# A graph-network kernel's edge loop rewritten: variance by cross terms, one vector pass, fp32 row strips, a ring of four halves, the reciprocal root on GpSimd

## The chip, the cores and the metric

The kernel runs on one core of one Trainium2 chip. The metric is device microseconds (us) of one execution. Two timed executions of the kernel before gave 4982.13 and 4989.26 us, median 4985.69 us.

Engines are called PE (TensorE matmul), PEld (its weight load), DVE (VectorE), ACT (ScalarE), POOL (GpSimd) and SP (SyncE, which issues DMAs).

## The reference, cut to what matters

Two message-passing layers over 12,500 nodes and 200,000 edges sorted by destination. The part that the change rewrites is the first layer's edge work:

```python
def _L0_gnn_ref(x, edge_index, edge_attr, W1, b1, g1, be1, W2, b2, Wu, bu, gu, beu):
    row, col = (edge_index[0], edge_index[1])
    msg_in = jnp.concatenate([x[row], edge_attr], axis=-1)      # 128 + 32 columns
    h = msg_in @ W1 + b1                                        # 256 columns
    h = jax.nn.gelu(_layernorm(h, g1, be1), approximate=False)
    msg = h @ W2 + b2
    agg = jax.ops.segment_sum(msg, col, num_segments=x.shape[0])
    u = jnp.concatenate([x, agg], axis=-1) @ Wu + bu
    u = jax.nn.gelu(_layernorm(u, gu, beu), approximate=False)
    return u + x
...
h = jnp.maximum(_layernorm(x, axis=-1), 0.0)
x = x + _L0_gnn_ref(h, edge_index, edge_attr_32, ...)
h = jnp.maximum(_layernorm(x, axis=-1), 0.0)
x = x + _L1_gnn_ref(h, edge_index, ...)                         # hypergraph layer
```

Since the message's second product is linear, the kernel sums gelu(layernorm(h)) per destination node and multiplies by W2 Wu afterwards.

## The kernel before, in words

The program is thirteen phases with a barrier between them: `setup_phase`, `node_tables`, `edge_messages`, `far_messages`, and so on up to `output_rows`. Each phase is written out by hand, engine by engine: every engine runs its instructions in the order of its block, and semaphores (`s_...`) order the engines against each other. No scheduler is involved.

`node_tables` works on 14 groups of 7 tiles of 128 nodes. It normalises x, multiplies by the x part of W1 (already centred, so that a row's mean is zero) and stores a table `p_tab` of 256 columns per node, which the edge loop gathers from. It also splits the 32 edge features (fp32) into three bf16 parts and stores them.

`edge_messages` is the edge loop. A tile is 128 edges, a **half** is 8 tiles, and there are 196 halves. For a half H, before the change:

- SP loads indices, digits and six bf16 blocks of edge features.
- POOL (`half`) gathers 8 x 128 rows of `p_tab` with 8 indirect DMAs (L561); every second gather waits until DVE has consumed the two tiles of the half before that stood in the same buffer (`s_add`). Between them it takes the power -0.5 of the variances, 128x8 (L567).
- PE (`product`) multiplies features by weights with two bf16 matmuls for a tile (L601, L602).
- DVE adds product and gathered rows (L752), scales by the root and g1 (L768) and adds be1 (L774).
- ACT squares and sums each tile for the variance (L674), applies gelu (L680) and builds one-hot masks for a histogram (L692 to L701).
- PE (`window_sums`, L623) multiplies the 256 hidden columns of a tile (as stationary operand, 128x128 fp32 twice) by a 128x32 one-hot mask of the destinations in a window of 32 nodes; DVE (`keep`, L791) adds the result to the sums in memory. PE also adds the histogram (L609).

The engines work on different halves at once: PE multiplies features of half H+1 while window sums of H-1 and H-2 run.

`node_update` (L1356 to L1474) multiplies the sums by W2 Wu, 14 groups of 7 tiles, and makes the second layer's input.

## Time and profile before

| what | us |
|---|---|
| median of 2 timed executions | 4985.69 |
| span of the profiled execution (the profile gives no other time of it) | 5038.3 |
| `setup_phase`, 0 to 39.6 | 39.6 |
| `node_tables`, to 346.8 | 307.2 |
| `edge_messages`, to 3111.5 | 2764.7 |
| far edges and degrees, to 3405 | 293.5 |
| `node_update`, to 3657 | 252.0 |
| the second layer, to the end | 1381.3 |

The profiled execution is one run and 52.6 us (1.1%) longer than the median of the timed ones. The stage bounds are read from the first and last instructions of each phase (the gathers of L561 begin at 346.8, the last `keep` ends with the loop at about 3111.5). Engine busy times are sums over a stretch; a wait that an engine spends for another is printed in brackets behind the instruction that ended it, with the line that released it. PEclk is the granted TensorE clock in parts of 2.4 GHz, so that 0.50 is its lower level of 1.2 GHz.

### The profile page before, as it was taken

The numbers are of one execution on the slowest core, as the hardware profiler recorded it, in microseconds if no ns is written. First come the engines' busy times: TensorE is split into PE (matmuls) and PEld (weight loads), VectorE is DVE, ScalarE is ACT, GpSimd is POOL, SyncE is SP. The second block draws the span as 40 slices with busy tenths as digits, with TensorE's granted clock in tenths as the row PEclk, the third lists the DMA queues.
The fourth block names the chain that finished last, engine by engine and source line by source line (L and its number), as shares of the span: only waits on it lengthen the run. The fifth ranks groups of instructions, "written<-read, shape, count | busy, mean of one in ns | idle before, by whom it ended". The sixth has DMA issues, their size and how long they took to land. (4 is left out here: it accounts for less than half of the span.)

```text
span 5038.3 us, 84982 instructions
## 1 busy us (share of the span) xinstructions
PE 3638.0 (72%) x16168; PEld 2611.6 (52%) x16168; DVE 2939.9 (58%) x8166; ACT 2492.2 (49%) x7380; POOL 3210.0 (64%) x2574
## 2 busy tenths in 40 slices
PE   3438999999999999999999997567633336666600
PEld 1216666666666666666666665565523324444300
DVE  6776776777777777767667775556811113323237
ACT  2437777777777777777777774462200001222200
POOL 2337777777777777777777774102366656888842
PEclk8665555555555555555555555555555555555555
DMA  6964444444444444444444442003311114555558
GB/s 249 343 242 113 117 117 112 115 114 114 117 112 116 113 116 115 114 114 115 111 112 113 116 113 61 12 15 95 101 49 47 44 38 80 75 74 78 74 124 222
DMA packets 726546, 557.03 MB, mean 111 GB/s; under 512 B 278174, under 2 KB 657170, under 8 KB 724594
## 3 DMA queue, kind: packets, MB, share of 16 engines
q0 software_dynamic: 135328, 250.63, 21.7%
q1 hardware_dynamic: 585138, 305.55, 21.4%
q10 hardware_dynamic: 6048, 0.52, 0.1%
q14 instruction: 24, 0.20, 0.0%
q8 instruction: 8, 0.13, 0.0%
HBM read 420.83 MB, written 135.45 MB: 110 GB/s over the span
## 5 line engine op out<-in xcount | busy, mean ns | idle before, releaser
L561 POOL DMA_INDIRECT stage<-p_tab,indices x1568 | 1761.6, 1123 | 660.3 <-issue 468.6
L674 ACT ACTIVATE table_weights_and_bias<-stage 128x256 bf16<-128x256 f32 x1568 | 632.4, 404 | 369.1 <-DVE stage L752 202.1
L768 DVE SCALAR_TENSOR_TENSOR stage<-stage,rstd,g 128x256 f32<-128x256 f32 x1568 | 653.9, 480 | 213.1 <-POOL rstd L567 213.1
L601 PE MATMUL ps_tiles<-edge_weights_a,edge_features_a 128*128 128x256 bf16 x1568 | 611.9, 390 | 201.1 <-DVE stage L752 156.4
L623 PE MATMUL ps_b<-window_mask,stage 128*128 128x32 f32 x3136 | 725.2, 402 | 2.9 <-ACT stage L680 2.9
L623 PEld LDWEIGHTS ps_b<-window_mask,stage 128*128 128x128 f32 x3136 | 698.3, 327 | 46.2 <-issue 43.3
L623 PE MATMUL ps_a<-window_mask,stage 128*128 128x32 f32 x3136 | 718.7, 400 | 1.9 <-ACT stage L680 1.7
L623 PEld LDWEIGHTS ps_a<-window_mask,stage 128*128 128x128 f32 x3136 | 706.8, 330 | 2.5 <-ACT stage L680 2.4
L602 PE MATMUL ps_tiles<-edge_weights_b,edge_features_b 64*128 64x256 bf16 x1568 | 614.4, 392 | 0.0
L752 DVE TENSOR_TENSOR stage<-ps_tiles,stage 128x512 f32<-128x512 f32 x784 | 538.1, 687 | 104.6 <-issue 101.2
L680 ACT ACTIVATE stage<-stage 128x1024 f32<-128x1024 f32 x392 | 414.2, 1057 | 366.8 <-DVE stage L774 332.5
L1713 POOL DMA_INDIRECT acc<-stage,target x320 | 502.6, 1571 | 105.7 <-ACT stage L1769 72.5
L774 DVE TENSOR_TENSOR stage<-stage,be 128x1024 f32<-128x1024 f32 x392 | 478.4, 1220 | 0.1
L692 ACT ACTIVATE high_mask<-iota,digits 128x98 bf16<-128x98 f32 x1568 | 436.8, 361 | 0.0
L601 PEld LDWEIGHTS ps_tiles<-edge_weights_a,edge_features_a 128*128 128x128 bf16 x1568 | 164.4, 105 | 484.4 <-issue 282.2
L1544 POOL DMA_INDIRECT stage<-xp_tab,indices x320 | 307.3, 960 | 160.1 <-issue 93.5
L741 DVE TENSOR_TENSOR window_mask<-iota,digits 128x256 f32<-128x256 f32 x196 | 83.4, 425 | 471.6 <-remote 376.7
L602 PEld LDWEIGHTS ps_tiles<-edge_weights_b,edge_features_b 64*128 64x128 bf16 x1568 | 158.7, 101 | 350.0 <-issue 350.0
L567 POOL TENSOR_TENSOR rstd<-var,minus_half 128x8 f32<-128x8 f32 x197 | 330.2, 1676 | 12.9 <-DVE var L760 8.6
L1763 ACT COPY sums<-ps_c 32x256 f32<-32x256 f32 x80 | 28.7, 358 | 547.6 <-PE ps_c L1733 543.4
L674 ACT ACTIVATION_READ_ACCUMULATOR table_weights_and_bias<-stage 128x1 f32 x1568 | 292.2, 186 | 0.0
L1560 PE MATMUL ps_a<-window_mask,stage 128*128 128x32 f32 x320 | 89.3, 405 | 256.7 <-DVE window_mask L1576 102.2
(258 smaller groups left out, 5413.2 us busy)
## 6 DMA issues: line engine op xcount, KB each, us to landing
edge_features_a<-ea_part SPq DMA_DIRECT2D x784, 64.0 KB
ea_part<-sums SPq DMA_DIRECT2D x42, 896.0 KB, 5.5
sums<-ea_d SPq DMA_DIRECT2D x14, 1792.0 KB, 9.2
stage<-p_tab,indices POOLq DMA_INDIRECT x1568
edge_features_b<-ea_part SPq DMA_DIRECT2D x392, 64.0 KB
acc<-zeros_bf SPq DMA_DIRECT2D x392, 64.0 KB
sums<-acc SPq DMA_DIRECT2D x56, 448.0 KB
sums<-src_d SPq DMA_DIRECT2D x46, 512.0 KB
```

What stands on the lines that cost most here:

```text
L561: gp.indirect_dma_start(out=rows[:, j, :], out_offset=None, in_=k.p_tab[:, :], in_offset=bass.IndirectOffsetOnAxis(ap=k.meta[h][:, j:j + 1 ...
L567: gp.tensor_tensor(k.rstd[i][:, :], k.var[i][:, :], k.neghalf[:, 0:HALF], ALU.pow)\
L601: nc.tensor.matmul(psH[q][:, t, :], k.eaA[h][:, e:e + P], k.wA[:, :], start=True, stop=False)
L602: nc.tensor.matmul(psH[q][:, t, :], k.eaB[h][:, e:e + P], k.wB[:, :], start=False, stop=True).then_inc(s_tile, 1)
L623: last = nc.tensor.matmul(psU[g][:, q, c, :], left, right, start=i == 0, stop=i == 1)
L674: nc.scalar.activation(k.scratch[:, j % GROUP, :], z[h][:, j, :], ACT.Square, scale=HID ** -0.5, accum_out=k.ssq[i][:, at:at + 1]).then_in ...
L680: nc.scalar.activation(part, part, ACT.Gelu).then_inc(s_gelu, 1)
L692: last = nc.scalar.activation(k.hi[h][:, j, :], k.iota[:, 0:NT], ACT.Square, bias=k.digits[h][:, 2 * HALF + j:2 * HALF + j + 1])
L752: v.tensor_tensor(z[h][:, 2 * q:2 * q + 2, :], psH[q], rows[:, 2 * q:2 * q + 2, :], ALU.add).then_inc(s_add, 1)
L768: o(v.scalar_tensor_tensor(z[h][:, j, :], z[h][:, j, :], root, k.g1[:, :], ALU.mult, ALU.mult))
L774: v.tensor_tensor(part, part, k.be1[:, :].unsqueeze(1).to_broadcast([P, GROUP, HID]), ALU.add).then_inc(s_z, 1)
L1713: gp.indirect_dma_start(out=k.acc[r], out_offset=bass.IndirectOffsetOnAxis(ap=k.target[h][:, j:j + 1], axis=0), in_=summed[:, r, :], in_of ...
```

## The change

The edge loop is rewritten on every engine, and tables and memory are laid out for it.

- **Cross terms.** The variance of a hidden row is split into a part of the node alone (computed in `node_tables` by ACT, and stored in `p_tab`), a cross term and a part of the features alone. `p_tab` grows from 256 to 292 columns (`PW`), and comes already multiplied by g1. PE multiplies features by a 128x128 block matrix (`feature_products`), DVE adds 32 gathered cross columns, multiplies by the features and reduces to 128x8 (`variance`). ACT's squares are gone from the edge loop.
- **One DVE pass.** The features are scaled by the root before the product (`scale_features`), turned on PE (`turn`), copied by ACT (`take_turned`), and multiplied by the weights (`feature_part`), where be1 is added as three bf16 parts. DVE then makes hidden = gathered row x root + product in one instruction a tile (`hidden`, L915).
- **fp32 row strips.** `feature_part` uses 32 of the array's 128 rows for a tile: four tiles stand on the four strips, fp32, with outputs in four PSUM banks. The bf16 parts of the features and their stores are gone from `node_tables`.
- **Ring of four halves.** The gathered rows have four buffers and hidden is written in place. A gather into a buffer waits for the window sums of the half four earlier (`s_seg`).
- **The root** is one power on POOL for each half (L645), and stands on POOL's queue behind the eight gathers of the half two later.
- Counts of edges for each node are taken as window counts, 0.0-cleared memory shrinks from three to two blocks, and `node_update` loses its one-row matmul for b2 and gets two POOL instructions a group in its place (`add_shift`).

```diff
+HALVES = 2 * BODIES
+RING = 4
+PW = HID + DE + 4
...
 def edge_messages(nc, k):
...
         @block.gpsimd
         def _(gp):
-            def half(b, h, lead):
-
-                H = 2 * b + h
-                wait_apart(k, gp, s_meta[h], 16 * b + 16)
+            def gather(b, r):
+                wait_apart(k, gp, s_meta[r], 16 * b + 16)
+                if from_first(b, 1):
+                    wait_apart(k, gp, s_seg, RING * b + r - 3)
                 for j in range(HALF):
-                    if j % 2 == 0 and not (lead and h == 0):
-                        wait_apart(k, gp, s_add, PH * (H - 1) + j // 2 + 1)
-                    if j == GROUP - 1 and not (lead and h == 0):
-                        rstd(H - 1, 1 - h)
-                    gather(h, j)
+                    gp.indirect_dma_start(out=rows[r][:, j, :], out_offset=None, in_=k.p_tab[:, :],
+                                          in_offset=bass.IndirectOffsetOnAxis(ap=k.meta[r][:, j:j + 1], axis=0))\
+                      .then_inc(s_g[r], 16)
+
+            def root(H, h):
+                gp.wait_ge(s_var, 2 * H + 2)
+                gp.tensor_tensor(k.rstd[h][:, :], k.var[h][:, :], k.neghalf[:, 0:HALF], ALU.pow).then_inc(s_root, 1)
+
+            for r in range(RING):
+                gather(0, r)
+                if r >= 2:
+                    root(r - 2, r % 2)
+            with gp.Fori(1, LAST + 1) as b:
+                for r in range(RING):
+                    gather(b, r)
+                    root(RING * b + r - 2, r % 2)
+            root(HALVES - 2, 0)
+            root(HALVES - 1, 1)
...
         @block.tensor
...
+            def turn(H, h):
+                pe.wait_ge(s_eas, H + 1)
...
+                for g in range(QUADS):
+                    last = nc.tensor.transpose(psT[:, g, :], k.eas[h][:, g * P:(g + 1) * P], k.ident[:, :])
+                last.then_inc(s_turn, 1)
...
+            def feature_part(H, h):
+                pe.wait_ge(s_ct, H + 1)
...
+                for g in range(QUADS):
+                    for i in range(GROUP):
+                        part = slice(DE * i, DE * (i + 1))
+                        nc.tensor.matmul(psE[i][:, g, :], k.easT[h][part, g, :], k.w1bg[part, :], start=True,
+                                         stop=False)
+                    for i in range(GROUP):
+                        part = slice(DE * i, DE * i + 3)
+                        last = nc.tensor.matmul(psE[i][:, g, :], k.ones_bf[part, :], k.bep[part, :], start=False,
+                                                stop=True)
+                last.then_inc(s_e, 1)
...
+            def window_sums(H, h, r):
+                pe.wait_ge(s_oh, H + 1)
...
+                for q in range(GROUP):
+                    for i in range(2):
+                        nc.tensor.matmul(psK[WIN * q:WIN * (q + 1), :], oh_bf[h][:, 2 * q + i, :],
+                                         k.ones_bf[:, 0:1], start=i == 0, stop=i == 1)
+                for q in range(GROUP):
+                    if q % 2 == 0:
+                        pe.wait_ge(s_gelu, 2 * H + q // 2 + 1)
+                    for c in range(2):
+                        for i in range(2):
+                            j = 2 * q + i
+                            last = nc.tensor.matmul(psW[:, q, c, :], rows[r][:, j, c * P:(c + 1) * P],
+                                                    k.oh[h][:, j, :], start=i == 0, stop=i == 1)
+                last.then_inc(s_seg, 1)
...
+            def slot(b, r):
+                H = RING * b + r
+                h, o = r % 2, 1 - r % 2
+                turn(H, h)
+                histogram(H - 1, o)
+                feature_part(H, h)
+                window_sums(H - 1, o, (r - 1) % RING)
+                window_counts(H - 2, h)
+                feature_products(H + 2, b + (r + 2) // RING, (r + 2) % RING)
...
         @block.scalar
...
+            def slot(b, r):
+                H = RING * b + r
+                h, o = r % 2, 1 - r % 2
+                gelu(H - 1, (r - 1) % RING, 1)
+                take_turned(H, h)
+                far_masks(H, h)
+                masks(H, h)
+                gelu(H, r, 0)
...
         @block.vector
...
+            def scale_features(H, r):
...
+                v.wait_ge(s_root, H + 1)
...
+                v.tensor_tensor(k.eas[h][:, :].rearrange("p (j f) -> p j f", f=DE), ea[r],
+                                k.rstd[h][:, :].unsqueeze(2).to_broadcast([P, HALF, DE]), ALU.mult).then_inc(s_eas, 1)
...
+            def slot(b, r):
...
+                variance(H + 1, b + (r + 1) // RING, (r + 1) % RING, H - 2, at)
+                window_masks(H, h)
+                low_masks(H, h)
+                count_masks(H - 2, h)
+                hidden(H, r, 0)
...
+                hidden(H, r, 7)
+                scale_features(H + 1, (r + 1) % RING)
```

(`wait_ge(s, n)` waits until semaphore `s` has reached `n`; `s_seg` reaches H+1 when the window sums of half H are done, `s_root` when its root is taken, `s_eas` when its features are scaled.)

**PE's queue in the edge loop.** Before, a stretch of one turn of the loop; `stage` is the hidden tile, `ps_tiles` the product, `ps_c` the histogram:

```order
L609 MATMUL ps_c<-high_mask,low_mask 128x98 x8
L614 ISA
L623 MATMUL ps_a<-window_mask,stage 128x32 x4
L623 MATMUL ps_a<-window_mask,ones_bf 128x32 x2
L623 MATMUL ps_a<-window_mask,stage 128x32 x4
L623 MATMUL ps_a<-window_mask,ones_bf 128x32 x2
L598 REGISTER_ALU
L601 MATMUL ps_tiles<-edge_weights_a,edge_features_a 128x256
L602 MATMUL ps_tiles<-edge_weights_b,edge_features_b 128x256
```

Now, one whole half:

```order
L678 MATMUL ps_a<-identity,features_scaled 128x128 x2
L724 MATMUL ps_c<-high_mask,low_mask 128x98 x8
L690 MATMUL ps_tiles<-edge_weights_scaled,features_turned 128x256 x4
L694 MATMUL ps_tiles<-shift_parts,ones_bf 128x256 x4
L690 MATMUL ps_tiles<-edge_weights_scaled,features_turned 128x256 x4
L694 MATMUL ps_tiles<-shift_parts,ones_bf 128x256 x4
L706 MATMUL ps_b<-ones_bf,window_mask 32x1 x8
L714 MATMUL ps_b<-window_mask,stage 128x32 x16
L731 MATMUL ps_c<-count_high_mask,count_low_mask 128x98
```

The sixteen bf16 products between the window sums are gone; all of a half's feature matmuls (of half H) now stand in one block ahead of all window sums (of half H-1), and the turn of the scaled features stands first.

**POOL's queue in the edge loop.** Before, with the waits named (the name is that of the semaphore's first owner; `xh_stored1` is here the hidden tiles' semaphore `s_add`, `features_loaded0` the variance's):

```order
L561 DMA stage<-p_tab,indices 128x256 [waits xh_stored1]
L561 DMA stage<-p_tab,indices 128x256
L64 REGISTER_ALU
L561 DMA stage<-p_tab,indices 128x256 [waits xh_stored1]
L566 REGISTER_ALU
L567 TENSOR_TENSOR rstd<-var,minus_half 128x8 [waits features_loaded0]
```

Now:

```order
L639 DMA stage<-p_tab,indices 128x292 [waits dst_loaded,windows_summed]
L639 DMA stage<-p_tab,indices 128x292 x7
L644 ISA
L645 TENSOR_TENSOR rstd<-var,minus_half 128x8 [waits edge_variance]
```

The wait moved from every second gather, on DVE's sum, to the first of eight, on PE's window sums, and the root moved from the middle of the gathers to behind all eight.

## Rows read from the trace of the kernel before

**Rows 1.** The page: granted TensorE clock in 40 slices, tenths of 2.4 GHz.
```profile
PEclk8665555555555555555555555555555555555555
```

**Rows 2.** Busy time by stage: stretch, length, engines, clock, DMA share, GB/s.
```profile
39.60:346.80 307.20, 134.97 (x295) 63.29 (x295) 224.12 (x449) 121.07 (x133) 95.90 (x29) 0.69 0.86 314
346.80:3111.50 2764.70, 2560.47 (x12545) 1839.88 (x12545) 1963.69 (x4706) 2032.59 (x6273) 2102.37 (x1766) 0.50 0.43 113
...
3405.00:3657.00 252.00, 184.16 (x588) 139.61 (x588) 189.32 (x686) 60.60 (x112) 71.88 (x42) 0.50 0.36 100
```

**Rows 3.** Groups in 450 to 3000 us, 183 halves: busy, mean ns, idle before.
```profile
L561 POOL DMA_INDIRECT stage<-p_tab,indices x1462 | 1645.2, 1125 | 593.7 <-issue 437.7 <-DVE stage L752 156.0
...
L623 PEld LDWEIGHTS ps_a<-window_mask,stage 128*128 128x128 f32 x2928 | 660.0, 330 | 0.1
L623 PEld LDWEIGHTS ps_b<-window_mask,stage 128*128 128x128 f32 x2928 | 652.0, 327 | 40.8 <-issue 40.8
L768 DVE SCALAR_TENSOR_TENSOR stage<-stage,rstd,g 128x256 f32<-128x256 f32 x1461 | 609.4, 480 | 197.6 <-POOL rstd L567 197.6
...
L601 PE MATMUL ps_tiles<-edge_weights_a,edge_features_a 128*128 128x256 bf16 x1460 | 569.7, 390 | 163.4 <-DVE stage L752 126.8 <-issue 32.2
...
L567 POOL TENSOR_TENSOR rstd<-var,minus_half 128x8 f32<-128x8 f32 x183 | 306.6, 1675 | 4.0
...
L609 PE MATMUL ps_c<-high_mask,low_mask 128*128 128x98 bf16 x1464 | 153.0, 281 | 0.0
...
L741 DVE TENSOR_TENSOR window_mask<-iota,digits 128x256 f32<-128x256 f32 x183 | 77.9, 425 | 448.2 <-remote 358.0 <-PE ps_b L623 88.7 <-issue 1.4
```

**Rows 4.** Timeline inside the edge loop: start, length, engine, line, [idle before].
```profile
1501.79 1.68 POOL L567 TENSOR_TENSOR rstd<-var,minus_half 128x8 f32<-128x8 f32 x1
...
1503.51 1.67 DVE L768 SCALAR_TENSOR_TENSOR stage<-stage,rstd,g 128x256 f32<-128x256 f32 x4 [2.07 <-POOL rstd L567]
...
1517.88 0.68 DVE L752 TENSOR_TENSOR stage<-ps_tiles,stage 128x512 f32<-128x512 f32 x1
...
1519.37 0.98 POOL L561 DMA_INDIRECT stage<-p_tab,indices  x1 [2.23 <-DVE stage L752]
```

**Rows 5.** Two lines' gathers: ns min/median/max, first and last start.
```profile
L561 POOL DMA_INDIRECT stage<-p_tab,indices x1568: 940/957/2036, 346.8 to 3088.2; - x196
...
L1544 POOL DMA_INDIRECT stage<-xp_tab,indices x320: 949/955/1195, 3664.0 to 4130.2; - x160
```

**Rows 6.** Timeline in `node_tables`: two transposes on PE; and ACT's copies in `node_update`.
```profile
49.22 0.47 PE L453 MATMUL ps_a<-identity,sums 128*128 128x128 f32 x1 [18.17 <-DVE sums L414]
49.48 0.42 PE L453 MATMUL ps_b<-identity,sums 128*128 128x128 f32 x1
...
L1356 ACT COPY stage<-sums x98: 493/511/513, 3405.9 to 3632.8; 128x384 f32 x84, 128x384 f32<-128x384 f32 x14
```

**Rows 7.** Other fp32 matmuls: a 32-row one and its successor, and the products at both clocks.
```profile
3121.24 1.21 PE L964 MATMUL ps_tiles<-edge_weights,stage 32*128 32x256 f32 x2 [10.37 <-DMA stage<-p_tab,stage]
3122.38 1.22 PE L965 MATMUL ps_tiles<-stage,identity 128*128 128x256 f32 x2
...
L459 PEld LDWEIGHTS ps_tiles<-table_weights_and_bias,sums x196: 186/314/338, 54.5 to 328.7; 128*128 128x128 f32 x196
L459 PE MATMUL ps_tiles<-table_weights_and_bias,sums x196: 486/844/1009, 54.5 to 329.0; 128*128 128x384 f32 x196
```

**Rows 8.** Groups of `node_tables` and `node_update`.
```profile
L392 DVE TENSOR_TENSOR sums<-sums 128x3584 bf16<-128x3584 f32 x14 | 54.5, 3892 | 17.0 <-ACT sums L439 17.0
L416 DVE TENSOR_TENSOR sums<-sums 128x3584 f32<-128x3584 f32 x14 | 54.4, 3884 | 5.1 <-ACT sums L433 5.1
...
L1388 PE MATMUL ps_tiles<-b2u,stage 1*128 1x128 f32 x164 | 64.9, 497 | 0.0
...
L1401 POOL TENSOR_TENSOR stage<-stage 128x896 f32<-128x896 f32 x13 | 27.9, 2149 | 45.7 <-ACT stage L1364 45.7
...
L1457 DVE TENSOR_TENSOR stage<-stage,beu 128x896 f32<-128x896 f32 x13 | 14.2, 1091 | 0.4
```

More of the change, by code:

```diff
@@ L605, in histogram @@
             def histogram(H, h):
+                if not inside(H):
+                    return
                 pe.wait_ge(s_lo, H + 1)
@@ L610, in histogram @@
                 last.then_inc(s_hist, 1)
-            def window_sums(gg, h, g, first):
-                pe.wait_ge(s_gelu, gg + 1)
-                if not first:
-                    pe.wait_ge(s_u, gg)
-                for q in range(2):
-                    for c in range(3):
-                        for i in range(2):
-                            j = GROUP * g + 2 * q + i
-                            left, right = ((z[h][:, j, c * P:(c + 1) * P], k.oh[h][:, j, :]) if c < 2 else
-                                           (k.ones_bf[:, :], oh_bf[h][:, j, :]))
-                            last = nc.tensor.matmul(psU[g][:, q, c, :], left, right, start=i == 0, stop=i == 1)
-                last.then_inc(s_seg, 1)
@@ L645, in _ @@
-            nc.tensor.matmul(psC, k.zerob[:, :], k.zerob[:, 0:NT], start=True, stop=False)
-            for q in range(PH):
-                product(0, 0, q, True)
-            for h in range(2):
-                slot(0, h, True)
-            with pe.Fori(1, BODIES - 1) as b:
-                for h in range(2):
-                    slot(b, h, False)
-            for h in range(2):
-                slot(BODIES - 1, h, False, ahead=h == 0)
-            window_sums(2 * (HALVES - 2) + 1, 0, 1, False)
@@ L662, in _ @@
+            slot(-1, 3)
+            for r in range(RING):
+                slot(0, r)
+            with pe.Fori(1, LAST) as b:
+                for r in range(RING):
+                    slot(b, r)
+            for r in range(RING):
+                slot(LAST, r)
+            slot(LAST + 1, 0)
+            slot(LAST + 1, 1)
+            nc.tensor.matmul(k.psC[:, 0:2 * NT], k.zerob[:, 0:P], k.zerob[:, 0:2 * NT], start=False, stop=True)\
+              .then_inc(s_hist, 1)
         @block.scalar
@@ L1232, in _ @@
             pe.sem_inc(s_mu, 2)
-            for t in range(HT):
-                last = nc.tensor.matmul(psD[:, t:t + 1], k.U[0:1, 2 * UCOLS + t * P:2 * UCOLS + (t + 1) * P],
-                                        k.ones[0:1, 0:1], start=True, stop=True)
-            last.then_inc(s_cnt, 1)
             with pe.Fori(0, n_bodies) as b:
```

1030 lines of the change are left out of this document (583 added, 447 removed).

## The prediction

> **What bounds the kernel now.** I read the stages first. The edge loop takes 2764.7 of 5038.3 us, with PE busy for 2560.5 of them at a granted clock of 0.50, that is 1.2 GHz [rows 1, 2]. It is where the change is, so the rest of the reading is there. Then the groups in a steady stretch, 450 to 3000 us, which holds 183 halves: 13.93 us a half [rows 3]. For a half, POOL spends 1645.2/183 = 8.99 us in eight gathers, 593.7/183 = 3.24 us in gaps before them and 1.68 us in the root: 13.9 us, the whole period. PE is busy for 2560.5/196 = 13.1 us of each [rows 2]. Both are nearly full, and they can be because they stand on different halves: POOL waits only for DVE's sum of two tiles (156.0 us in all 183 halves), never for PE's window sums. The kernel's period is now the work of the fullest engine. What matters is whether the change keeps it so.
>
> **The change, and the circle in it.** I followed the new order of POOL and PE for one half H, and it closes:
> 1. PE ends the window sums of H-1. The gathers of H+3 go into the same buffer and wait for exactly that.
> 2. POOL issues eight gathers, and only behind them takes the root of H+1.
> 3. DVE's `scale_features(H+1)` waits for the root, PE's `turn(H+1)` for DVE, ACT's copy for the turn, PE's `feature_part(H+1)` for the copy.
> 4. PE's window sums of H stand behind `feature_part(H+1)` on PE's queue. Back to 1, one half later.
>
> So no two of these steps overlap, and the period of a half is their sum instead of the fullest engine. The terms, one after the other:
> - From the wait to the first gather: DVE's sum ends at 1517.88 + 0.68 = 1518.56, the gather that it frees starts at 1519.37 [rows 4]: 0.81 us.
> - Eight gathers. The median in the edge loop is 957 ns and the mean 1125; in the second layer, where DVE has little to do, the median is 955 with rows half as wide [rows 3, 5]. So the width of the row (292 for 256 columns) should cost POOL nothing, and in the new loop DVE idles during the gathers: 8 x 0.957 = 7.66 us, and seven gaps at the 'issue' mean of 437.7/1462 = 0.30 us [rows 3]: 2.10 us.
> - The root: 1.68 us, and 0.04 us to DVE [rows 4].
> - `scale_features`, 128x256: as L741, 0.43 us [rows 3]. To PE 0.06 us (my choice; the transposes' row shows its wait only).
> - Two transposes: 49.22 to 49.90, 0.68 us [rows 6]. The copy of 128x256 then takes under the 0.51 us of 128x384 [rows 6], but the histogram, between turn and feature part on PE, covers it with 153.0/183 = 0.84 us [rows 3].
> - `feature_part`: eight fp32 products of 32 rows and 256 columns and eight bf16 ones. This is the term that the trace doesn't show. A lone 32-row fp32 product (two records) takes 1.21 us, and the next starts 1.14 us after it [rows 7]. If four strips ran fully side by side, two groups would cost 2 x (1.21 + 0.39), the last for the bf16 set by L601's mean [rows 3]: 3.2 us. If nothing overlapped, 8 x 1.14 for fp32 and 8 x 0.39: 12.2 us, an upper end, since 1.14 holds a start from standstill. Between them stands the pace at which PE loads fp32 weights, (660.0 + 652.0)/5856 = 0.224 us a record [rows 3]: 16 x 0.224 + 8 x 0.1 = 4.4 us. I take 4.4, since the new products have the same loads as L623 and would have to wait for them even with four strips free.
> - Window sums: eight tiny bf16 counts, at most the histogram's 0.84, I take 0.8; then the same 32 fp32 records as before, 32 x 0.224 = 7.17 us, and 0.2 us until the last has drained.
>
> Sum: 0.81 + 7.66 + 2.10 + 1.68 + 0.04 + 0.43 + 0.06 + 0.68 + 0.84 + 4.4 + 0.8 + 7.37 = **26.9 us a half**, against 13.93. PE waits through the first 12.8 us of it, but for some small products.
>
> The Trainium skill ("TensorE: Matmul & The Clock Gate", Part 3, on row/col tiling) reports 3.07x for four 32-row tiles side by side. By that, feature_part would take 12.2/3.07 = 4.0 us, the half 26.5 us and the kernel 7310 us. The rows show no strips side by side: by them alone it could be 12.2 us, 34.7 us a half and 8890 us.
>
> What else stands in the half is covered. DVE's variance of H+1, masks and keeps (an estimate of 5 us, at 0.43 for each pass of 128x256 [rows 3]) stand before `hidden(H)`, which takes 8 x 0.48 = 3.8 us [rows 3]; both run under the window sums and the gathers, and the gelu of H is needed only by the next window sums, a circle later. ACT loses its squares. `feature_products` and the counts run during the gathers. SP loads indices and features of H+4 a whole turn ahead. The rewrite's gain, less DVE and ACT work, is thus off the path; if the circle went, PE's own work would be late next.
>
> **The edge loop.** Window sums of half 0 end after 32 gathers (40.2 us), two roots (3.4) and the rest of the chain (14.6): 58 us. Then 192 halves with a gather in the circle, 192 x 26.9 = 5165 us, and 48 us for the last three without gathers, 16 each. 5271 us, against 2764.7: **+2506**.
>
> **Other stages.** `node_tables` loses the splitting of features, 54.5 + 54.4 us of DVE [rows 8] and about two thirds of its DMA traffic (share 0.86 [rows 2]), and gains a multiplication of 128x1792, priced as twice the 128x896 of L1457: 2 x 1.09 x 14 = 31 us [rows 8], and squares on ACT. The wait of DVE on PE and POOL then sets the pace: I take 15.5 us a group for 307.2/14 = 21.9, -90 us (-150 if DVE's own work were all, -30 if the waits grow). Setup gets more small DMAs and products, +8 (0 to 20). `node_update` loses a third matmul, at most 64.9/82 = 0.79 us a tile [rows 8], and gains two POOL instructions of 2.15 us a group [rows 8] before DVE's sum; POOL is busy for 71.9 of 252.0 us [rows 2], so they fit: -15 (-50 to +40). Together -97.
>
> **The sum.** 5038.3 + 2506 - 97 = 7447 us against the profiled execution's own span. The timed executions' median lies 52.6 us under that span; I take that off unchanged: **7390 us**, 48% slower. Two in a hundred is what a measurement of this kernel can tell from no change.
>
> **Rivals.**
> - *Strips don't overlap.* feature_part takes up to 12.2 us: 192 x 7.8 = +1500, 8890 us. For it: a 32-row product takes as long as a 128-row one, 1.21 and 1.22 us [rows 7], and nothing in the trace runs side by side. Against: four strips have separate rows and banks. Chance 0.09.
> - *The clock rises.* In `node_tables`, with 384-column fp32 products, the granted clock averages 0.69 at a PE that is busy less than half of the time; in the edge loop it is 0.50 at 93% busy [rows 1, 2]. Products of 256 fp32 columns might raise it again. L459's matmuls take 486 ns at the upper level and 844 at the median, its loads 186 and 314 [rows 7], about 0.6; PE's part of the circle, 14.1 us, would shrink by 5.7 us, 192 x 5.7 = 1090: 6300 us. Chance 0.09. The Trainium skill (same page, Part 1, the clock gate) says that sustained activity releases the full clock and idling withdraws it. By that rule the loop before should run at 2.4 GHz, and this trace disagrees (0.50); for the new loop, with PE idle for almost half of each period, it points at 1.2 GHz.
> - *The circle is open* (not slower). If the gathers of H+3 found their buffer free before POOL came to them, the period would be PE's own work: 0.68 + 0.84 + 4.4 + 0.8 + 7.37 + about 1.0 for the products and counts = 15.1 us, or 13.9 with strips side by side; then 192 x 0 to 1.2 - 97 gives 4890 to 5120 us. It decides at 14.4 us a half: under it the saving of the other stages pays. Against it: the wait is for half H-1 and there is no earlier event. Chance 0.03.
> - *The gathers stay at their mean of 1.125 us*, 28.2 us a half, 7650 us. This is part of the forecast's case.
>
> Forecast 0.77 (range of its own 7050 to 7800), strips 0.09, clock 0.09, open circle 0.03, something else 0.02. The range of 8 in 10 is 6650 to 8200: it cuts off the clock case and the strips case, and takes in a half 3.9 us shorter or 4.2 us longer than mine, so feature_part's lower end of 3.2 us and most of the way to its upper one. Faster by over 2%: 0.02; within 2%: 0.01; slower: 0.97.
>
> **What would show it.** In the profile after: POOL's first gather of each half waits for PE's `window_sums` line, seven more follow with gaps of 0.30 us, and the root starts right behind the last; DVE's longest wait is for the root, before `scale_features`; PE is busy for about half of the stage, with its longest wait, 12 to 13 us, before the turn; the granted clock is 0.50; the half takes 26.9 us. The products of `feature_part` show by their starts whether strips overlap. The prediction is wrong if the root is taken earlier than the last gather, if PE's wait is for ACT or the keeps instead, or if the period is under 20 us.

## Result, and the profile after

The changed kernel takes **6839.89 us** (two executions, 6836.68 to 6843.1) against 4985.69 before: 1.3726 times as long [1.3696, 1.3756]. 7390 was forecast, with a range of 6650 to 8200; the measured time lies in it, 550 us (7%) below the forecast. The profiled execution's own time is 6843.1 us and its span 6841.3, so for this kernel span and time agree.

Busy time by stage of the changed kernel (columns as in [rows 2]):

```profile
248.10:4919.50 4671.40, 2341.52 (x15483) 2035.87 (x15483) 1361.09 (x5095) 1442.16 (x3333) 1832.16 (x1764) 0.50 0.26 68
4919.50:6841.30 1921.80, 842.67 (x3088) 645.62 (x3088) 768.53 (x2995) 326.84 (x970) 1066.04 (x792) 0.52 0.37 74
```

The edge loop went from 2764.7 us [rows 2] to 4671.4, +1906.7. It begins at 248.1 where it began at 346.8, and what follows it takes 1921.8 us where 5038.3 - 3111.5 = 1926.8 us stood: the other stages give 104 us back, 98 of them in `node_tables` (209.1 us, from 39 to 248.1, for 307.2). PE was busy for 93% of the loop and is for 50%; the granted clock is 0.50 as before. No engine is full.

The costliest groups of the page, which answer to [rows 3] (busy, mean ns | idle before, by releaser; here over the whole span):

```profile
L639 POOL DMA_INDIRECT stage<-p_tab,indices x1568 | 1503.9, 959 | 2816.1 <-PE ps_b L714 2354.5
L678 PE MATMUL ps_a<-identity,features_scaled 128*128 128x128 f32 x392 | 134.7, 447 | 2315.7 <-DVE features_scaled L876 2315.7
L876 DVE TENSOR_TENSOR features_scaled<-edge_features,rstd 128x256 f32<-128x256 f32 x196 | 83.3, 425 | 2983.6 <-POOL rstd L645 2965.6
```

Read the releasers as a ring: POOL waits for PE's window sums (L714), DVE for POOL's root, PE for DVE's scaled features. Before, POOL waited 156.0 us in 183 halves, and for DVE [rows 3]; now it waits 2354.5 us in 192, 12.26 us each. The gathers' mean fell from 1125 to 959 ns, beside their old median of 957 [rows 5].

One turn of that ring in the timeline of the changed kernel (start, length, engine, line, [idle before]):

```profile
3005.45 1.02 POOL L639 DMA_INDIRECT stage<-p_tab,indices  x1 [12.26 <-PE ps_b L714]
3006.77 0.96 POOL L639 DMA_INDIRECT stage<-p_tab,indices  x1 [0.30 <-issue]
...
3014.34 0.95 POOL L639 DMA_INDIRECT stage<-p_tab,indices  x1 [0.30 <-issue]
3015.30 1.68 POOL L645 TENSOR_TENSOR rstd<-var,minus_half 128x8 f32<-128x8 f32 x1
3017.01 0.43 DVE L876 TENSOR_TENSOR features_scaled<-edge_features,rstd 128x256 f32<-128x256 f32 x1 [15.48 <-POOL rstd L645]
...
3017.50 0.69 PE L678 MATMUL ps_a<-identity,features_scaled 128*128 128x128 f32 x2 [11.81 <-DVE features_scaled L876]
...
3017.97 0.86 PE L724 MATMUL ps_c<-high_mask,low_mask 128*128 128x98 bf16 x8
...
3018.76 0.52 PEld L690 LDWEIGHTS ps_tiles<-edge_weights_scaled,features_turned 32*128 32x128 f32 x8
3018.77 1.24 PE L690 MATMUL ps_tiles<-edge_weights_scaled,features_turned 32*128 32x256 f32 x8
3018.95 0.42 DVE L848 TENSOR_TENSOR cross_terms<-ps_d,stage 128x256 f32<-128x256 f32 x1 [1.51 <-issue]
...
3019.78 0.44 PE L694 MATMUL ps_tiles<-shift_parts,ones_bf 3*128 3x256 bf16 x4
...
3019.99 1.08 PE L690 MATMUL ps_tiles<-edge_weights_scaled,features_turned 32*128 32x256 f32 x8
...
3020.77 0.15 DVE L839 COPY window_count<-ps_b 128x1 f32<-128x1 f32 x1
...
3020.85 0.44 PE L694 MATMUL ps_tiles<-shift_parts,ones_bf 3*128 3x256 bf16 x4
...
3021.21 0.15 PEld L706 LDWEIGHTS ps_b<-ones_bf,window_mask 128*32 128x32 bf16 x8 [0.62 <-DVE window_count L839]
3021.21 0.23 PE L706 MATMUL ps_b<-ones_bf,window_mask 128*32 128x1 bf16 x8
...
3021.38 7.03 PE L714 MATMUL ps_b<-window_mask,stage 128*128 128x32 f32 x32
...
3029.24 1.02 POOL L639 DMA_INDIRECT stage<-p_tab,indices  x1 [12.26 <-PE ps_b L714]
```

From one first gather to the next it is 3029.24 - 3005.45 = 23.79 us. Each row starts where the one before it in the ring ends: the period is a sum, as the prediction had it, and the terms can be read off as differences of starts (they stand in a table further down). Of the 191 periods of the whole loop, from the first gather that waits on, 172 are 23.7 or 23.8 us, one is 24.0, 16 are 25.2 or 25.3 and two are 20.9.

### The profile page after: what moved, and what is told of

It reads as the page before. It is cut to its first block and busy times, and to the rows that moved or that the text cites. A ratio compares the mean times of both kernels' runs of the same rounds, so it can differ in the third digit from the quotient of the medians.

```text
span 6841.3 us, 78884 instructions
## 1 busy us (share of the span) xinstructions
PE 3314.1 (48%) x18894; PEld 2741.1 (40%) x18894; DVE 2310.1 (34%) x8581; ACT 1840.9 (27%) x4600; POOL 2984.2 (44%) x2602
## 5 line engine op out<-in xcount | busy, mean ns | idle before, releaser
L639 POOL DMA_INDIRECT stage<-p_tab,indices x1568 | 1503.9, 959 | 2816.1 <-PE ps_b L714 2354.5
L714 PE MATMUL ps_b<-window_mask,stage 128*128 128x32 f32 x6272 | 1370.2, 400 | 0.0
L714 PEld LDWEIGHTS ps_b<-window_mask,stage 128*128 128x128 f32 x6272 | 1343.8, 330 | 2.9
L915 DVE SCALAR_TENSOR_TENSOR stage<-stage,rstd,ps_tiles 128x256 f32<-128x256 f32 x1568 | 630.4, 476 | 13.1 <-remote 10.8
L690 PE MATMUL ps_tiles<-edge_weights_scaled,features_turned 32*128 32x256 f32 x3136 | 451.4, 669 | 0.5 <-issue 0.5
L645 POOL TENSOR_TENSOR rstd<-var,minus_half 128x8 f32<-128x8 f32 x196 | 328.3, 1675 | 17.1 <-DVE var L866 12.7
L786 ACT ACTIVATE low_mask<-iota,digits 128x128 bf16<-128x128 f32 x784 | 248.0, 389 | 0.0
L690 PEld LDWEIGHTS ps_tiles<-edge_weights_scaled,features_turned 32*128 32x128 f32 x3136 | 212.1, 319 | 80.3 <-issue 52.0
L667 PE MATMUL ps_d<-edge_weight_products,edge_features 128*128 128x128 f32 x784 | 232.7, 453 | 13.6 <-DVE cross_terms L848 10.7
L1746 PE MATMUL ps_a<-window_mask,stage 128*128 128x32 f32 x320 | 90.6, 406 | 223.1 <-issue 82.7
L667 PEld LDWEIGHTS ps_d<-edge_weight_products,edge_features 128*128 128x128 f32 x784 | 187.4, 329 | 14.8 <-issue 11.6
L848 DVE TENSOR_TENSOR cross_terms<-ps_d,stage 128x256 f32<-128x256 f32 x196 | 83.3, 425 | 290.7 <-issue 285.2
```

What stands on the lines that cost most here:

```text
L639: gp.indirect_dma_start(out=rows[r][:, j, :], out_offset=None, in_=k.p_tab[:, :], in_offset=bass.IndirectOffsetOnAxis(ap=k.meta[r][:, j:j ...
L645: gp.tensor_tensor(k.rstd[h][:, :], k.var[h][:, :], k.neghalf[:, 0:HALF], ALU.pow).then_inc(s_root, 1)
L667: last = nc.tensor.matmul(psF[:, g * P:(g + 1) * P], eaT[r][:, g, :], k.gblk[:, :], start=True, stop=True)
L690: nc.tensor.matmul(psE[i][:, g, :], k.easT[h][part, g, :], k.w1bg[part, :], start=True, stop=False)
L714: last = nc.tensor.matmul(psW[:, q, c, :], rows[r][:, j, c * P:(c + 1) * P], k.oh[h][:, j, :], start=i == 0, stop=i == 1)
L786: last = nc.scalar.activation(k.lo[h][:, j, :], k.iota[:, :], ACT.Square, scale=-1.0, bias=k.digits[h][:, HALF + j:HALF + j + 1])
```

## The experiments

The first measurement was on a chip where the kernel before takes 4985.69 us. The first four experiments ran where it takes 4788.44, the next four where it takes 4787.2. In that second set the changed kernel itself ran again, as the base for all of them; the base for the first four (root_first, two_roots, one_strip, sums_first) is so a run on another chip, on which the kernel before agrees within 0.03%.

**after_again**: the changed kernel, unedited.

> The changed kernel itself, unedited, as the base for the runs beside it. Its first measurement was 6839.89 us against 4985.69 before, a ratio of 1.3726, and on the chip of the other experiments the kernel before took 4788.44 us, so this should stand between 1.3726 x 4788 = 6573 and 6840 us. The half's period should be 23.8 us with POOL waiting about 12.3 us of each for PE's window sums.

6774.95 us (6763.41 to 6776.86), ratio 1.4145 [1.4121, 1.4169], period 23.73 to 23.80 us. The changed kernel is 65 us faster on this chip, the kernel before 198 us: the ratio moved by the kernel before, not by the changed one.

**root_first**: the order of POOL turned round.

```diff
             for r in range(RING):
-                gather(0, r)
                 if r >= 2:
                     root(r - 2, r % 2)
+                gather(0, r)
             with gp.Fori(1, LAST + 1) as b:
                 for r in range(RING):
-                    gather(b, r)
                     root(RING * b + r - 2, r % 2)
+                    gather(b, r)
```

> Only POOL's queue changes: the root of half H+1 stands ahead of the eight gathers of H+3 instead of behind them. Theory (the circle): window sums of H-1, then eight gathers, then the root, then scale, turn, feature part, then window sums of H make a chain of one half, 23.8 us. With the root ahead of the gathers the chain is open, and the period is that of the fullest engine: PE's own work in the profile after, 0.69 + 0.58 + 2.5 + 0.2 + 7.03 + 0.27 + 1.19 = 12.5 us, or POOL's, eight gathers at 0.96 to 1.125 us with gaps of 0.30, a root of 1.68 and a restart of 0.83, 12.3 to 13.6 us. 13.3 us a half gives 6840 - 192 x 10.5 = 4825 us (4700 to 4950). Rival 1: the extra time lies in the new PE and DVE work, then under 100 us change. Rival 2: the gathers themselves must follow the window sums and hold up the variance, then the half stays above 20 us and the time above 6100 us.

**4478.17 us** (4476.43 to 4482.14), ratio to before 0.9349 [0.9333, 0.9365]. Nothing was made cheaper, two calls changed places, and 2297 us went, more than the 1890 to 2140 that the expected 4700 to 4950 us stood for. The waits of root_first in 1000 to 2500 us (in total, times, longest), some 126 halves:

```profile
ACT features_turned L774 <- PE ps_a L678: 457.3, 126, 4.8
DVE features_scaled L876 <- POOL rstd L645: 439.7, 125, 4.7
POOL stage L639 <- issue: 310.0, 999, 1.8
...
POOL stage L639 <- PE ps_b L714: 1.8, 6, 0.3
```

POOL's wait for PE went from 760.5 us in 62 halves, in the same stretch of the changed kernel, to 1.8 us. The period is 11.9 us (11.95 in the mean of 191; the expectations of the later runs put it at 11.74): eight gathers with their gaps and the root fill it, 1185.56 us busy and 310.0 in gaps of 1500. The stretch itself:

```profile
1000.00:2500.00 1500.00, 1339.75 (x9927) 1161.88 (x9925) 868.19 (x3274) 925.08 (x2141) 1185.56 (x1130) 0.57 0.52 135
```

PE is busy for 89% of it, at a mean clock of 0.57: part of the time it runs at 2.4 GHz. A window sum of 32 records takes 7.03 us at 1.2 GHz, and here in some halves:

```profile
2006.19 4.16 PE L714 MATMUL ps_b<-window_mask,stage 128*128 128x32 f32 x32
```

**root_mid**: the root between the fourth and the fifth gather.

```diff
                 for j in range(HALF):
+                    if j == GROUP and root_of is not None:
+                        root(root_of, r % 2)
                     gp.indirect_dma_start(...)
```

> The root of H+1 is taken between the fourth and the fifth gather of H+3, not behind the eighth. Circle theory (the period is the sum of the steps between one window sum's end and the next, and the gathers ahead of the root are among them): four gathers and four gaps of 1.26 us leave the circle, 4 x 1.26 = 5.0 us of 23.8, so 192 x 5.0 = 970 us under the changed kernel, period 18.7 us; the four gathers behind the root run beside PE's chain and cost nothing. Rival (it is the amount of POOL's work, whatever its order): no change, within 20 us. Rival (root_first gained because the clock rose, and the order only lets it rise): a jump at some point and not a line, so more than 970 us with PEclk over 0.52, or nothing.

5669.78 us (5665.46 to 5672.86), ratio 1.1841 [1.1822, 1.1861], so -1105 us against after_again. Most periods are 18.64 to 18.68 us, that is 5.1 us less than 23.77, against 5.0 expected. Of 191 periods, 41 are some 2.9 us shorter than the others, nearly all of them 15.7 to 15.8 us, with window sums at the upper clock:

```profile
3004.52 0.95 POOL L641 DMA_INDIRECT stage<-p_tab,indices  x1 [7.11 <-PE ps_b L713]
...
3009.29 1.67 POOL L647 TENSOR_TENSOR rstd<-var,minus_half 128x8 f32<-128x8 f32 x1
3010.99 0.43 DVE L875 TENSOR_TENSOR features_scaled<-edge_features,rstd 128x256 f32<-128x256 f32 x1 [10.31 <-POOL rstd L647]
3011.14 1.17 POOL L641 DMA_INDIRECT stage<-p_tab,indices  x1 [0.18 <-issue]
...
3015.21 4.28 PE L713 MATMUL ps_b<-window_mask,stage 128*128 128x32 f32 x32
3020.30 0.94 POOL L641 DMA_INDIRECT stage<-p_tab,indices  x1 [4.23 <-PE ps_b L713]
```

The last four gathers now run beside PE's chain. 192 x 5.1 = 980 us of the gain are the gathers that left the ring. The other 125 are what the clock gave: 2.9 us for each half that got it, with a mean granted clock of 0.52 for 0.50. The rival that the clock is the cause falls: 192 x 41/191 x 2.9 = 120 us is what it can account for, while the 5.1 us stand in the halves at 1.2 GHz too.

**two_roots** and **power_in_wait**: one more power for each half, behind the gathers (in the ring) or ahead of the wait (outside it). The lines of power_in_wait are shown without its semaphore and one power ahead of the loop.

```diff
 two_roots, in root:
...
                 gp.wait_ge(s_var, 2 * H + 2)
+                gp.tensor_tensor(k.w_row[h][:, :], k.var[h][:, :], k.neghalf[:, 0:HALF], ALU.pow)
                 gp.tensor_tensor(k.rstd[h][:, :], k.var[h][:, :], k.neghalf[:, 0:HALF], ALU.pow).then_inc(s_root, 1)
...
 power_in_wait, in gather:
...
                 if from_first(b, 1):
+                    gp.wait_ge(s_fill, RING * (b - 1) + r + 1)
+                    gp.tensor_tensor(k.w_row[0][:, :], k.ones[:, 0:HALF], k.neghalf[:, 0:HALF],
+                                     ALU.pow).then_inc(s_fill, 1)
                     wait_apart(k, gp, s_seg, RING * b + r - 3)
```

> Each root is taken twice on POOL (the first result goes to a buffer that the edge loop does not use). A dose for the root on the circle: +1.68 us on each of 192 halves, +320 us, 7160 us. If POOL's power were covered by other engines' work: no change.

> One more power of the same shape (128x8, its result unused) for each half on POOL, but ahead of the wait for the window sums, where POOL stands idle for 12.26 us. Circle theory: nothing, within 20 us, since POOL is idle there and the step isn't in the circle; the wait shrinks from 12.3 to about 10.6 us. Rival (POOL's amount of work decides, or the power disturbs DVE through a shared resource): +1.67 x 192 = +320 us, as much as the same power costs when taken behind the gathers or more.

two_roots: 6926.97 us (6920.28 to 6933.67), +152 us; power_in_wait: 6749.89 (6744.93 to 6751.91), -25 us. The same work costs something in one place and nothing in the other, so it isn't POOL's amount of work. Behind the gathers it lengthens an ordinary period from 23.77 to 25.36 us, 1.6 us, the power's own length:

```profile
3004.72 1.68 POOL L645 TENSOR_TENSOR w_row<-var,minus_half 128x8 f32<-128x8 f32 x1
3006.38 1.64 POOL L646 TENSOR_TENSOR rstd<-var,minus_half 128x8 f32<-128x8 f32 x1
```

Ahead of the wait it only shortens the wait, from 12.25 us:

```profile
3010.16 1.02 POOL L643 DMA_INDIRECT stage<-p_tab,indices  x1 [10.64 <-PE ps_b L719]
```

Why then 152 and not 192 x 1.6 = 307 us? Of 191 periods of two_roots, 49 are 22.3 to 22.9 us, up to 2.9 below the rest: the upper clock again. 192 x 49/191 x 2.9 = 143 us come back, which leaves 164, near the 152 measured. The -25 us of power_in_wait, 5 more than its expectation allowed, are of the same kind: 8 of its 191 periods are 20.8 us, and one of after_again's is short, at 22.2; 8 x 2.9 = 23. A step added to the ring was priced rightly by its length, and a second effect hid half of it.

**one_strip**: all 16 products of the feature part on rows 0 to 31 of the array (the features of the wrong tile go in for three of four tiles, in the same amount).

```diff
-                        part = slice(DE * i, DE * (i + 1))
+                        part = slice(0, DE)
...
-                        part = slice(DE * i, DE * i + 3)
+                        part = slice(0, 3)
```

> The products of feature_part all use array rows 0 to 31 (and rows 0 to 2 for the bf16 part) instead of four different strips; every tile of a group so gets the first one's features, and all other work is as before. If four strips run side by side, the block of eight fp32 and eight bf16 products grows from 2.5 us to 16 x 0.43 + 8 x 0.21 = 8.5 us; 0.6 us of that is covered by PE's wait for DVE, so +5.4 us a half, +1040 us, 7880 us. If the strips did not overlap and the block was short for another reason: no change.

8024.43 us (8023.02 to 8025.85), ratio 1.6755 [1.6721, 1.6788]: +1249 us against after_again, period 30.1 to 30.2 us for 23.77. PE's rows:

```profile
3016.70 3.06 PEld L690 LDWEIGHTS ps_tiles<-edge_weights_scaled,features_turned 32*128 32x128 f32 x8
3016.71 3.78 PE L690 MATMUL ps_tiles<-edge_weights_scaled,features_turned 32*128 32x256 f32 x8
...
3020.28 1.06 PE L694 MATMUL ps_tiles<-shift_parts,ones_bf 3*128 3x256 bf16 x4
...
3021.13 3.62 PE L690 MATMUL ps_tiles<-edge_weights_scaled,features_turned 32*128 32x256 f32 x8
...
3024.55 1.06 PE L694 MATMUL ps_tiles<-shift_parts,ones_bf 3*128 3x256 bf16 x4
```

Four products take 3.78 us on one strip and 1.24 us on four. The part takes 25.53 - 16.71 = 8.8 us for 2.4. Strips do run side by side, 3.05 times as fast. The expectation was 1040 us, because it put the part at 8.5 us and took 0.6 of that to be hidden in a wait of PE for DVE; the period grew by the whole 6.4 us, so nothing was hidden (early_starts, below, shows that there was no such wait).

**sums_first**: window sums ahead of turn, histogram and feature part on PE.

```diff
                 H = RING * b + r
                 h, o = r % 2, 1 - r % 2
+                window_sums(H - 1, o, (r - 1) % RING)
                 turn(H, h)
                 histogram(H - 1, o)
                 feature_part(H, h)
-                window_sums(H - 1, o, (r - 1) % RING)
```

> Only PE's queue changes: the window sums of H-1 stand ahead of turn, histogram and feature part of H. If the circle ran through the feature part alone, as the prediction had it, ahead of the window sums would now be neither turn nor feature part, 3.8 us a half less: 6110 us. The profile after shows a second path beside it: PE waits 0.62 us for DVE's window_count (L839) before the counts, and DVE reaches that copy only after the scaling, a register load of 1.51 us and 2.0 us of variance and keeps. If this path closes the circle as well, nothing is won: 6840 us, within 60. Engines in parallel (no circle): no change either, but then root_first would change nothing.

6737.86 us (6737.27 to 6738.46), ratio 1.4068 [1.404, 1.4096]: -37 us against after_again. That is the case in which nothing is won; the 6840 us of the expectation were the first chip's. The ring has a second closing link, and it took over:

```profile
3022.20 0.42 DVE L876 TENSOR_TENSOR features_scaled<-edge_features,rstd 128x256 f32<-128x256 f32 x1 [5.46 <-POOL rstd L645]
3023.96 0.42 DVE L848 TENSOR_TENSOR cross_terms<-ps_d,stage 128x256 f32<-128x256 f32 x1 [1.33 <-issue]
...
3025.78 0.15 DVE L839 COPY window_count<-ps_b 128x1 f32<-128x1 f32 x1
...
3025.98 0.23 PE L706 MATMUL ps_b<-ones_bf,window_mask 128*32 128x1 bf16 x8 [11.33 <-DVE window_count L839]
```

The window sums need an empty PSUM tile; DVE empties it in `keep`, and the keeps stand behind `scale_features` on DVE's queue, so behind the root. From the scaled features to PE's counts it is 25.98 - 22.20 = 3.78 us on this way, and 21.21 - 17.01 = 4.20 us on PE's way in the changed kernel. The mean period fell from 23.88 to 23.63 us.

**early_starts**: DVE loads the window positions (four registers a half; the expectation says eight) ahead of scaling.

```diff
                 at = starts(H - 2) if inside(H - 2) else None
+                scale_features(H, r)
                 variance(H + 1, ...)
...
                 hidden(H, r, 7)
-                scale_features(H + 1, (r + 1) % RING)
```

> DVE loads the eight window positions (registers) of the keeps ahead of scaling the features, while it waits for the root, and no longer behind it. Nothing else moves. In the changed kernel PE waits 0.62 us at the window counts for DVE's last keep, and DVE's path from the scaled features to that keep begins with 1.51 us in which it only loads registers. Theory (two paths lead from the scaled features to the window sums, PE's and DVE's, and DVE's is the longer by 0.62 us): the load leaves the path, PE's own turn, histogram and feature part bind, and the half gets 0.6 us shorter, 192 x 0.62 = 120 us less (80 to 130), PE's wait at the counts goes to nearly nothing. Rival (PE's wait there is only a name and its own products would not have ended before): 0, within 20 us.

6753.3 us (6751.85 to 6758.52), ratio 1.4104 [1.4081, 1.4128]: -22 us, not -120. The ordinary period stays at 23.8 us (six periods of 191 are short by the upper clock, for one in after_again). My theory that DVE's way was 0.62 us the longer falls. DVE's last keep ends 9.56 - 7.26 = 2.30 us after the scaling began, for 3.91 before, and PE starts the counts no earlier: its 0.62 us stay, under another name.

```profile
3007.26 0.42 DVE L876 TENSOR_TENSOR features_scaled<-edge_features,rstd 128x256 f32<-128x256 f32 x1 [16.27 <-POOL rstd L645]
...
3009.41 0.15 DVE L839 COPY window_count<-ps_b 128x1 f32<-128x1 f32 x1
3011.46 0.15 PEld L706 LDWEIGHTS ps_b<-ones_bf,window_mask 128*32 128x32 bf16 x8 [0.62 <-issue]
```

Again it is 11.46 - 7.26 = 4.20 us to the counts. PE's way binds, by 0.3 us over DVE's (20.77 + 0.15 against 21.21). The 0.62 us before the counts aren't a wait for DVE, though the profile of the changed kernel had put them down to it. They are idle time of the weight load alone: PE's own products run on through them, the last set of L694 in the changed kernel from 3020.85 to 3021.29 us, and the load for the counts starts at 3021.21, as that set ends. Why it doesn't start earlier is open.

**root_first_again**, **first_and_early** and **first_two_roots** ran together on one more chip, where the kernel before takes 4915.88 us. The edits are the ones above, made to root_first.

> The root ahead of the gathers, as in root_first, once more as the base for the two runs beside it: 4478 us, 0.935 of the kernel before, period 11.74 us.

> The root ahead of the gathers, and DVE's loads of the window positions ahead of scaling the features. POOL theory (the period of 11.74 us is POOL's own work: eight gathers with their gaps, 10.1 us, and the root, 1.68): no change, within 10 us, for DVE's 1.48 us of loads lie beside it. Rival (PE's work, 10.7 us of 11.7 at a clock of 0.57, with its waits for DVE, sets the period): up to 0.5 us less a half, 95 us.

> The root ahead of the gathers and taken twice (the first result unused). POOL theory: the whole second root is paid, 1.64 x 192 = +315 us, period 13.4 us, 4790 us in all, and no part of it comes back through the clock, since PE isn't in the sum. Behind the gathers the same second root lengthened the ordinary halves by 1.6 us too, but some halves came out 2.9 us shorter and the kernel paid only 152 us. Rival (PE binds at its clock): less than half of it, under 160 us.

| kernel | us | ratio to before |
|---|---|---|
| root_first_again | 5301.56 (5297.9 to 5310.02) | 1.0794 [1.0775, 1.0813] |
| first_and_early | 5291.15 (5284.79 to 5299.94) | 1.0763 [1.0745, 1.0781] |
| first_two_roots | 5306.29 (5302.06 to 5313.37) | 1.0803 [1.0785, 1.0821] |

All the expectations missed: the base itself took 823 us more than in root_first, with a mean period of 15.9 us for 11.95, and is slower than the kernel before. So the two runs beside it say nothing on what fills the period of 11.9 us, which stays as the trace of root_first tells it (POOL). The waits of root_first_again in 1000 to 2500 us, 94 halves:

```profile
ACT stage L766 <- DVE stage L915: 676.5, 174, 7.9
DVE stage L915 <- remote: 673.6, 86, 8.3
POOL stage L639 <- PE ps_b L714: 399.8, 87, 5.6
PEld ps_b L714 <- issue: 389.0, 503, 1.9
```

In root_first there was no remote wait, and 2.2 us before L714's loads. Here in nearly every half DVE stands for 673.6/86 = 7.8 us before the hidden rows, for something that the profile only calls remote, while PE's window sums come one record at a time. PE and DVE in one half:

```profile
2003.85 2.40 PE L714 MATMUL ps_b<-window_mask,stage 128*128 128x32 f32 x10
...
2007.41 0.40 PE L714 MATMUL ps_b<-window_mask,stage 128*128 128x32 f32 x1 [1.16 <-issue]
...
2008.97 0.21 PE L714 MATMUL ps_b<-window_mask,stage 128*128 128x32 f32 x1 [1.17 <-issue]
...
2011.93 4.07 PE L714 MATMUL ps_b<-window_mask,stage 128*128 128x32 f32 x19 [1.22 <-issue]
...
2012.06 3.22 DVE L915 SCALAR_TENSOR_TENSOR stage<-stage,rstd,ps_tiles 128x256 f32<-128x256 f32 x8 [7.48 <-remote]
```

Both engines come free together: in 173 of the 178 such waits of the loop DVE goes on 0.1 us after the last of PE's late records, as in these rows (2012.06 and 2011.93). DVE's only semaphore there, that of the feature part's products, had been reached long before (2003.76), so this looks like one stall of two engines and not like DVE waiting for a result.

The second root of first_two_roots is hidden there, since POOL waits for PE in any case: its wait falls from 399.8/87 = 4.6 us to 251.2/86 = 2.9. The kernel before has waits of the same name in its own trace: 358.0 us before L741 [rows 3]. The changed kernel has one, of 10.8 us before its first hidden rows, on the first chip and none on its second. One run was kept to ask whether the two go together.

**root_first_third**: once more, on one more chip.

> The root ahead of the gathers, unedited, on one more chip. It took 4478 us beside a kernel before of 4788 us, and 5302 us beside one of 4916 us. Theory (chips are of two kinds, and the kernel before shows by its own time which it is on): where the kernel before takes 4787 to 4790 us this one takes 4470 to 4490 us (ratio 0.935), and DVE waits for nothing outside the core before the hidden rows; where the kernel before takes 4900 us or more it takes 5200 us or more, with some 7.7 us of such a wait in each half. Rival (the two times of this kernel have nothing to do with that of the kernel before): any other pairing.

4477.63 us (4476.54 to 4478.36) beside 4786.1 us before, ratio 0.9353 [0.9338, 0.9369], with the waits and the clock (0.57) of the first time and nothing remote. The pairing held: where the kernel before takes 4786 to 4788 us, root_first takes 4478; where it takes 4916, 5302. With three chips that is a pattern and no proof. What the remote wait is, wasn't settled: it comes on some chips, to an instruction that the profile shows nothing else to wait for, in kernels whose gathers run beside window sums and DVE's passes (before, root_first), and hardly where they take turns (the changed kernel). Whether the overlap is its cause wasn't tried. On the chip of the first measurement, whose kernel before takes 4986 us and shows the remote wait, root_first wasn't run, and by this pattern it would not win there.

## Why the prediction was right, and what was mis-sized

**The mechanism held at each step.** The first gather of each half waits for PE's L714, seven follow with gaps of 0.30 us, the root starts behind the last, DVE's longest wait is for it, PE's is 11.81 us before the turn, PE is busy for 50%, the clock is 0.50. root_first shows, on the two chips where the kernel before takes 4786 to 4788 us, that the ring is the whole loss: with one link opened the kernel is 6.5% faster than before, so there the rewrite's work is worth having. It doesn't show it everywhere: where the kernel before takes 4916 us the opened kernel is 8% slower, with the stall of two engines in place of the ring. The chip of the first measurement is more like that one, by its time (4986 us) and by the remote waits of the kernel before, and how much of the 37% would be left there with the ring open wasn't measured.

**The terms** (us a half, from the turn above, in starts and ends):

| step | forecast | measured |
|---|---|---|
| restart of POOL | 0.81 | 0.83 |
| gathers and gaps | 9.76 | 9.85 |
| root, and to DVE | 1.72 | 1.71 |
| scale, and to PE | 0.49 | 0.49 |
| turn | 0.68 | 0.47 |
| histogram | 0.84 | 0.80 |
| feature_part | 4.4 | 2.44 |
| counts | 0.8 | 0.17 |
| window sums | 7.37 | 7.03 |
| **sum** | **26.9** | **23.79** |

What came from rows of the same instruction (gathers, root, passes) was within 0.1 us. Three sizes were off:

- **feature_part**, 2.0 of the 3.1 us. I bounded it by 3.2 and 12.2 and chose 4.4, on the ground that weight loads of L623's pace, 0.224 us a record, would have to be waited for even with four strips free. They are not: one 32-row load takes 0.28 to 0.33 us in both kernels, and eight of them stand in 0.52 us on four strips and in 3.06 on one, so they overlap as well. Even the lower end, 3.2, was too high. It counted a lone product's 1.21 us and 0.39 us behind it, while the second group starts 1.22 us after the first, and the bf16 set begins before it. The 2.44 measured also end with the load of the counts, which starts only as the last set ends. The upper end of 12.2 was too high too: on one strip the part takes 8.8 us, since 1.14 us between two lone products held a start from standstill. The Trainium skill's ratio ("TensorE: Matmul & The Clock Gate", Part 3) of 3.07 for four strips, given for products of 512 columns, agrees here with 256: 3.78/1.24 = 3.05. I applied it to 12.2 where 8.8 was the time of one strip; 8.8/3.07 = 2.9 would have been nearer than my 4.4.
- **Counts**, 0.6. I took the histogram's 0.84 us as a bound for eight products and went to it. Eight products of one column take 0.17.
- **Turn and sums**, 0.2 and 0.3. The second transpose overlaps the histogram's first load, and the last product's drain was counted in the sums and again as 0.2 us (the restart of POOL already runs from the end of the last record).

192 x 3.1 = 595 us of the 600 by which the loop came out shorter than 5271. The forecast's range took in only half of the way to the 12.2 us of the strips' rival (4.4 + 4.2 = 8.6), not most of it.

**The other stages** were forecast at -97 us and came at -104: -98 for -90 in `node_tables`, -1 for +8 in the setup, and -5 for -15 in all that follows the loop.

**The base.** I took 52.6 us off, because the profiled execution of before was longer than the timed ones. That was an execution's own excess and didn't carry over: the span after is within 2 us of the time. 5038.3 + 1906.7 - 103.7 = 6841.3 needs no such term. That it brought the forecast nearer, to 7390 from 7447, was luck.

**The rivals.** Strips don't overlap: refuted by one_strip, at 8.8 us for the part where the rival had 12.2. The clock rises: not in this kernel (0.50), but it did where the ring was shortened or stretched, in single halves, at 2.9 us each. The rule of the Trainium skill that the prediction cites (the same page, Part 1, the clock gate) has sustained activity release the full clock. The loop before, 93% busy at 0.50, disagrees, and root_first, busy for 89%, is granted 0.57. For the changed loop, half idle at 0.50, the trace agrees. Circle open: refuted for this order, and root_first shows its price. It was put at 4890 to 5120 us, 0.98 to 1.03 of the kernel before; opened, it is 4478 us (0.935) on two chips and 5302 (1.079) on a third. The estimate missed on both sides: it had PE's work as the period, 13.9 to 15.1 us, while the strips and the clock made that 10.7 us a half (1339.75 us in 125.6 halves) and POOL's 11.9 us set the period; and the remote waits weren't foreseen. **What I left out**: the second closing link, by the keeps, at 3.78 us against 4.20. It changed nothing here, but it would have made "let PE sum first" look like a cure, and it isn't.

## What to carry to other kernels

When an in-order queue gets a new wait, write down who needs what stands behind it, and follow that back to the wait. If it closes, the period is the sum of the links, however idle each engine looks, and the cheapest cure is to move the link, not to speed it up: here two calls changed places, for 2297 us of 6775 on two of three chips. Price each link by a row of the same instruction; for one that has no such row, ask what overlaps inside it before taking a lone instruction's pace. And a kernel that fills its engines should be timed on more than one chip: one order won by 6.5% on two and lost by 8% on a third.

## What the runs showed of the hardware

- Four fp32 products of 32 rows and 256 columns, on four strips of the array: 1.24 us at 1.2 GHz; on one strip 3.78 us. Their eight weight loads take 0.52 us on four strips and 3.06 us on one.
- The clock came back for single halves (2.9 us less of 25.4) in 49 of 191 periods of two_roots, where PE is busy for less of the time (686.71 of 1500 us) than in the changed kernel (751.76), which got it in two of 191. Some of that gap is the shorter records of the fast halves themselves. A step of 1.6 us cost 152/192 = 0.8 in the mean. Why one half gets the upper clock and the next doesn't is open: power_in_wait has the same PE work and the same period as after_again and got it in 8 halves, after_again in one.
- Loading four registers on DVE holds up the next pass by 1.3 to 1.5 us, which DVE's busy time doesn't show (93.8 us before L848 in 63 halves of the changed kernel); moved into a wait it costs nothing (early_starts).
- The same kernel took 4478, 4478 and 5302 us on three chips, each within 0.3% of itself.
